# The bias of v added by a matmul in the keys phase of a two-layer gated cross-attention kernel

## The reference

```
x = x + tanh(g_xattn[0]) * attention0(layernorm(x), ctx)     # 16 heads of 16, with biases
    kh = split_heads(ctx @ w_k.T + b_k)
    vh = split_heads(ctx @ w_v.T + b_v)                       # <- this bias
x = x + tanh(g_ffn[0])   * experts(layernorm(x))
x = x + tanh(g_xattn[1]) * attention1(layernorm(x), ctx)      # 16 heads of 64, no biases
x = x + tanh(g_ffn[1])   * prototypes(layernorm(x))
```

## Time and profile before

| what | value |
|---|---|
| runs, median (lowest to highest) | 3129.29 us (3127.91 to 3131.58) |
| profiled execution: span from first to last instruction | 3124.2 us |
| what lies around the span, against the median | 5.1 us |
| keys phase, from the start of the span to the first load of the next phase | about 527 us |
| one quiet group, from v step to v step | 45.9 us |
| one noisy group | 48.4, 51.4 and 49.1 us |

### The profile page before, as it was taken

The page is one execution under the profiler, slowest core; times in us unless marked ns, Lnnn a source line. Parts: engine busy times, 40 slices in busy tenths (PEclk is TensorE's granted clock), DMA queues, the critical chain, the costliest instruction groups (busy, mean ns, idle before and its releaser), DMA issues.

```text
span 3124.2 us, 101333 instructions
## 1 busy us (share of the span) xinstructions
PE 2797.3 (90%) x33450; PEld 2225.3 (71%) x33450; DVE 2640.9 (85%) x6703; ACT 1875.0 (60%) x3733; POOL 2190.1 (70%) x3924
## 2 busy tenths in 40 slices
PE   4889896788888888869899999999999999999997
PEld 2444444666666666647688888888888888888886
DVE  6887886888888888875699999998989988999986
ACT  2666765777777777775455545555545555555553
POOL 3892001666667666645488888888888888888887
PEclk9999998999999999989999999999999999999999
DMA  5987666232223222623444444444444344444441
GB/s 153 361 332 289 244 243 227 73 86 79 73 78 83 80 74 77 224 82 81 96 104 111 107 101 95 104 104 95 101 91 97 94 103 104 96 98 93 108 94 43
DMA packets 367621, 388.79 MB, mean 124 GB/s; under 512 B 118432, under 2 KB 341264, under 8 KB 362320
## 3 DMA queue, kind: packets, MB, share of 16 engines
q1 hardware_dynamic: 346960, 335.42, 38.9%
q0 software_dynamic: 7328, 23.40, 2.4%
q10 hardware_dynamic: 12960, 25.23, 2.2%
HBM read 235.08 MB, written 148.83 MB: 123 GB/s over the span
## 4 chain that ended last, share of the span: by engine, by line
PE 39%; DVE 6%; issue 3%; POOL 2%; ACT 2%; DVEq 0%; POOLq 0%; ACTq 0%
PE banks L150 11%; PE banks L152 11%; PE banks L151 10%; PE banks L1310 2%; PE banks L1295 2%; DVE a_probT_lo L1397 1%; PE banks L1342 1%; ACT a_qT_hi L1199 1%; DVE a_pick L1522 1%; DVE a_y L1541 1%; DVE a_rsum L1409 1%; PE banks L1365 1%; DVE a_wsel L1531 0%; PE banks L1357 0%; ACT a_ynT_hi L1199 0%
## 5 line engine op out<-in xcount | busy, mean ns | idle before, releaser
L1199 ACT ACTIVATE a_qT_hi<-banks 128x512 f16<-128x512 f32 x252 | 150.5, 597 | 700.8 <-PE banks L152 700.8
L383 POOL TENSOR_TENSOR a_probT_lo<-a_expT,a_probT_hi 128x512 f16<-128x512 f32 (+1 forms) x384 | 372.0, 998 | 243.7 <-ACT a_probT_hi L458 243.7
L449 ACT ACTIVATE a_expT<-banks,a_top,w_score_scale 128x512 f32<-128x512 f32 (+1 forms) x384 | 272.2, 709 | 111.4 <-PE banks L544 111.2
L1112 POOL TENSOR_TENSOR a_pn<-a_prob,a_rsum 128x1024 f32<-128x1024 f32 (+1 forms) x256 | 307.2, 1221 | 5.8 <-DVE a_rsum L1411 5.3
L150 PE MATMUL banks<-a_xnT_hi,w_q_hi 128*128 128x256 f16 x1024 | 281.6, 275 | 4.7 <-DVE a_xnT_lo L1395 3.0
L150 PE MATMUL banks<-a_vo_front,a_probT_hi 128*128 128x256 f16 x1024 | 278.9, 272 | 2.7 <-DVE a_probT_lo L1397 2.6
L152 PE MATMUL banks<-a_xnT_hi,w_q_lo 128*128 128x256 f16 x1024 | 280.9, 274 | 0.0
L151 PE MATMUL banks<-a_xnT_lo,w_q_hi 128*128 128x256 f16 x1024 | 280.9, 274 | 0.0
L152 PE MATMUL banks<-a_vo_front,a_probT_lo 128*128 128x256 f16 x1024 | 279.0, 273 | 0.0
L151 PE MATMUL banks<-a_vo_front,a_probT_hi 128*128 128x256 f16 x1024 | 279.0, 272 | 0.0
L1397 DVE SCALAR_TENSOR_TENSOR a_probT_lo<-banks,a_probT_hi 128x512 f16<-128x512 f32 (+1 forms) x384 | 212.6, 582 | 35.7 <-ACT a_probT_hi L1199 35.3
(11 more groups left out here) (400 smaller groups left out, 10655.0 us busy)
## 6 DMA issues: line engine op xcount, KB each, us to landing
vo<-kv_vo_out SPq DMA_DIRECT2D x38, 2048.0 KB, 7.6
a_vo_front<-vo SPq DMA_DIRECT2D x128, 512.0 KB
kt<-kv_k_out ACTq DMA_DIRECT2D x9, 2560.0 KB, 15.0
a_k<-kt SPq DMA_DIRECT2D x64, 308.0 KB, 3.5
kv_raw_e<-in_L_ffn_w POOLq DMA_DIRECT2D x16, 1024.0 KB, 9.7
a_x<-in_x SPq DMA_DIRECT2D x64, 256.0 KB
a_y<-in_x SPq DMA_DIRECT2D x64, 256.0 KB, 2.8
x<-a_y SPq DMA_DIRECT2D x64, 256.0 KB, 2.2
```

What stands on the lines that cost most here:

```text
L383: pool.tensor_tensor(probT[b][1][0:rows, first:end, :], expT[b][0:rows, first:end, :], probT[b][0][0:rows, first:end, :], ALU.subtract).th ...
L449: act.activation(expT[1 - h][0:rows, first:end, :], bank, ACT.Exp, bias=top[0:rows, 0:1], scale=weights["score_scale"][0:rows, 0:1]).then_ ...
L1112: last = pool.tensor_tensor(keys_of(pn[h]), keys_of(prob_of(u, h, 2)), rsum[h][:, :].unsqueeze(2).broadcast_to([P, H, n]), ALU.mult)
L1199: act.activation(out, bank[:, 0:cols].rearrange("p (c s) -> p c s", c=out.shape[1]), ACT.Copy, scale=scale)\
```

## The change

The bias row is split once into float16 halves and put on partitions 0 (hi) and 32 (lo) of a tile `bias_parts` of 64 partitions. A second tile `pick_bias` is zero but for ones in rows 0 and 32. For each chunk a seventh matmul, `pick_bias` against `bias_parts`, with a contraction of 64 rows and 256 columns, is accumulated in the same bank, and only it signals that the bank is full. `v_sum`, its semaphore and L2279 go. ACT copies the bank, and DVE subtracts from the bank. The bank is free when the lo half is done. On DVE at the start of the phase two small operations and two waits are added; on POOL three memsets, with waits, ahead of the memset of `v_out`. PE waits once, at the first chunk of group 0, for both tiles.

```diff
-        nc.vector.tensor_scalar(bv[:, :], bv[:, :], out_inverse[:, WV:WV + 1], None, ALU.mult)
+        step(nc.vector.tensor_scalar(bv[:, :], bv[:, :], out_inverse[:, WV:WV + 1], None, ALU.mult))
+        step(nc.vector.tensor_copy(bias_parts[:, :], bv[0:64, :]))
+        nc.vector.tensor_tensor(bias_parts[32:64, :], bv[32:64, :], bias_parts[32:64, :], ALU.subtract)\
+            .then_inc(bias_ready, 1)
...
+        pool.memset(pick_bias[:, :], 0.0).then_inc(pick_zero, 1)
+        pool.wait_ge(pick_zero, 1)
+        for n, r in enumerate((0, 32)):
+            pool.memset(pick_bias[r:r + 1, :], 1.0).then_inc(pick_set, 1)
+            pool.wait_ge(pick_set, n + 1)
...
                 for c in range(DC):
-                    last = matmul3(nc, bank[0:m, 0:D], [x[:, c, a * P:a * P + m] for x in rowsT[p]],
-                                   [x[:, c, :] for x in wv], c == 0, c == DC - 1)
-                filled(last, g, ("v", a))
+                    matmul3(nc, bank[0:m, 0:D], [x[:, c, a * P:a * P + m] for x in rowsT[p]],
+                            [x[:, c, :] for x in wv], c == 0, False)
...
+                filled(nc.tensor.matmul(bank[0:m, 0:D], pick_bias[:, 0:m], bias_parts[:, :], start=False, stop=True),
+                       g, ("v", a))
...
-                need(act, v_sum_ready, g * CH + a + 1)
-                act.activation(v_out[p][0:m, a, :, :, D // H:2 * (D // H)], by_head(v_sum[0:m, :]), ACT.Copy)\
+                act.activation(v_out[p][0:m, a, :, :, D // H:2 * (D // H)], by_head(full(g, ("v", a))[0:m, 0:D]), ACT.Copy)\
                     .then_inc(v_hi, 1)
...
-                nc.vector.tensor_tensor(v_sum[0:m, :], full(g, ("v", a))[0:m, 0:D], bv[0:m, :], ALU.add)\
-                    .then_inc(v_sum_ready, 1)
-                need(dve, v_hi, at + 1)
-                need(dve, v_sum_ready, at + 1)
-                nc.vector.tensor_tensor(v_out[p][0:m, a, :, :, 0:D // H], by_head(v_sum[0:m, :]),
+                bank = full(g, ("v", a))
+                need(dve, v_hi, g * CH + a + 1)
+                nc.vector.tensor_tensor(v_out[p][0:m, a, :, :, 0:D // H], by_head(bank[0:m, 0:D]),
                                         v_out[p][0:m, a, :, :, D // H:2 * (D // H)], ALU.subtract).then_inc(v_ready, 1)
```

More of the change, by code:

```diff
@@ L1859, in keys_values_phase @@
     vT = [sb(f"vT_{n}", [P, PAIRS, BANK], F16) for n in ("hi", "lo")]
-    v_sum = sb("v_sum", [P, D])
+    bias_parts, pick_bias = sb("bias_parts", [2 * 32, D], F16), sb("pick_bias", [2 * 32, P], F16)
+    pick_zero, pick_set, bias_ready = sem("pick_zero"), sem("pick_set"), sem("bias_ready")
     work = [psum[:, s * BANK:(s + 1) * BANK] for s in range(BANKS)]
@@ L1865, in keys_values_phase @@
     vo_stored = [sem(f"vo_stored{p}") for p in range(2)]
-    rowsT_hi, rowsT_ready, k_ready, v_sum_ready, v_hi, v_ready = (
-        sem("rowsT_hi"), sem("rowsT_ready"), sem("k_ready"), sem("v_sum_ready"), sem("v_hi"), sem("v_ready"))
+    rowsT_hi, rowsT_ready, k_ready, v_hi, v_ready = (
+        sem("rowsT_hi"), sem("rowsT_ready"), sem("k_ready"), sem("v_hi"), sem("v_ready"))
     k_hi = sem("k_hi")
@@ L1928, in freed @@
             return vo_ready, (g * CH + use[1]) * PAIRS + use[2] + 1
-        return v_sum_ready, g * CH + use[1] + 1
+        return v_ready, g * CH + use[1] + 1
     def groups(eng, body):
@@ L2108, in body @@
                 for c in range(DC):
-                    last = matmul3(nc, bank[0:m, 0:D], [x[:, c, a * P:a * P + m] for x in rowsT[p]],
-                                   [x[:, c, :] for x in wv], c == 0, c == DC - 1)
-                filled(last, g, ("v", a))
+                    matmul3(nc, bank[0:m, 0:D], [x[:, c, a * P:a * P + m] for x in rowsT[p]],
+                            [x[:, c, :] for x in wv], c == 0, False)
+                if isinstance(g, int) and g == 0 and a == 0:
+                    pe.wait_ge(bias_ready, 1)
+                    pe.wait_ge(pick_set, 2)
+                filled(nc.tensor.matmul(bank[0:m, 0:D], pick_bias[:, 0:m], bias_parts[:, :], start=False, stop=True),
+                       g, ("v", a))
         first_tensor(pe)
@@ L2276, in body @@
             for a, m in enumerate(chunks(g)):
-                at = g * CH + a
-                need(dve, v_ready, at)
-                nc.vector.tensor_tensor(v_sum[0:m, :], full(g, ("v", a))[0:m, 0:D], bv[0:m, :], ALU.add)\
-                    .then_inc(v_sum_ready, 1)
-                need(dve, v_hi, at + 1)
-                need(dve, v_sum_ready, at + 1)
-                nc.vector.tensor_tensor(v_out[p][0:m, a, :, :, 0:D // H], by_head(v_sum[0:m, :]),
+                bank = full(g, ("v", a))
+                need(dve, v_hi, g * CH + a + 1)
+                nc.vector.tensor_tensor(v_out[p][0:m, a, :, :, 0:D // H], by_head(bank[0:m, 0:D]),
                                         v_out[p][0:m, a, :, :, D // H:2 * (D // H)], ALU.subtract).then_inc(v_ready, 1)
```

## The result

Seven runs of the changed kernel took 3134.81 to 3142.57 us, with a median of 3136.78 us; seven runs of the kernel before took 3121.75 to 3131.58, with a median of 3129.29. The medians are 7.5 us apart and the means 9.8. The ratio of the runs is 1.0032, with a 95% interval of 1.0021 to 1.0042: **the kernel became slower by 10.0 us (6.6 to 13.1)**. The forecast was 3134.1 us, that is +4.8. The time lies in the range given (3125 to 3141), but "same" (within 6.3 us) was given the highest chance, 0.55, and the result is beyond that mark. So the sign of the sum was right and its size about half.

A forecast was written before the change was run, and what follows sets the result against it. PE was taken as the path through v and vT, with DVE pacing the product stage. 7.9 - 0.9 - 1.3 - 1.0 + 0.1 = +4.8 us on the median 3129.3 gave 3134.1 us, range 3125 to 3141.

The forecast's parts named there:

- PE is the path from v to vT: In quiet groups' v steps, PE sets the pace and DVE's relief counts nothing; 1.31 us added per four-chunk step.
- The price of a change of height: On PE around each bias matmul, switching between 64 and 128 rows costs 0.109 us each, 0.327 per matmul.
- The rival without such a price: On PE, bias matmuls cost columns only, 3.9 instead of 11.8 us: -3.1, 3126.2 us; chance 0.17.
- DVE's stall in the noisy groups: In three groups beside POOL's work, DVE's late subtract loses 4.8 us, which the change removes; net -0.9 after bias matmuls.
- The rival of the stores: In noisy groups, store waits take back the gain: +7.0 to +10.9 us, 3136.3 to 3140.2; chance 0.30.
- noisy v stretches: Three groups beside POOL's work, v to first product split: 4.8 us gained, 3.9 of bias matmuls added, net -0.9.
- The clock: In two noisy groups, PE's clock stops falling once PE no longer waits for DVE: -1.3 us, half of 2.6.
- The tail: In the last group, the v store goes out earlier, with the last vo store as limit: -1.0 us.
- The start: At the phase's start, bias scaling and two small DVE operations mostly fit where DVE was idle: +0.1 us.
- quiet groups: Six groups with four chunks each, where bias matmuls lie wholly on PE's path: +7.9 us, period 45.9 to 47.2.

The follow-up runs named there:

- e2: The changed kernel without its bias matmul, DVE's and ACT's side kept: 3128.78 us, ratio 0.9995 to the kernel before.
- e3: The changed kernel with the bias matmul contracting 128 rows instead of 64, extra picking rows zero: 3132.05 us, ratio 1.0005 to the kernel before.
- e4: The changed kernel with a second 64-row matmul, adding zero, ahead of each chunk's six: 3146.23 us, ratio 1.0056 to the kernel before.
- e7: The kernel with v's bias folded once into the output bias, without adds, buffer or bias matmuls: 3126.97 us, ratio 0.9992 to the kernel before.
- e10: The kernel before again, unedited, timed and profiled: 3125.73 us, ratio 0.9999.
- e11: The kernel before again, unedited, for a third profile: 3126.77 us in one run.
- e5: The kernel before, DVE's add and buffer kept, plus a 64-row matmul adding zero in each chunk: 3137.72 us, ratio 1.0032.
- e1: The changed kernel once more, unedited: 3139.45 us, ratio 1.0033 to the kernel before.
- e6: The changed kernel with a group's bias matmuls in a row ahead of its v matmuls: 3136.45 us, ratio 1.0027 to the kernel before.
- e12: The kernel with v's bias folded into the output bias, unedited, profiled a second time: 3122.76 us in one run.

## Why the prediction was half right

**PE is the path from v to vT: right.** Each of the six quiet stretches grew with what PE got, 7.65 us in all (106.67 - 99.02 in the two traces), with 7.9 forecast; the period came out at 47.18 against 47.2. DVE's whole relief moved no quiet group: 99.0 in e2 as in the kernel before.

**The price of a change of height: right.** 0.21 + 0.21 = 0.42 us around a bias matmul where 0.11 + 0.11 would stand, so 0.10 for each change and 0.315 for the chunk; 0.109 and 0.327 were taken from the earlier trace rows. e3 takes the changes away and keeps the columns, e4 doubles the matmuls but not the changes, and both times follow (7.4 us less with 8 expected, 6.8 more with 6 expected). The rival without such a price (3126.2 us) is out.

On this the Trainium skill, "TensorEngine Tiling (Array Packing)", Key Properties, says that a change of tiling mode drains the engine. The trace agrees in that no weight load runs under the matmul before it there, and gives 0.10 us as the size of a change here. The rule that a matmul with few rows takes as long as a full one ("TensorE: Matmul & The Clock Gate", Why this matters for your kernels) holds for the two 64-row matmuls side by side in e4 (0.12 us) and misleads for one that stands alone between others: 0.315 us.

**DVE's stall in the noisy groups: gone, as forecast, but worth less than was put down.** It was put at -4.8 us, which against 3.9 us of bias matmuls left a net of -0.9. The stall went: L2291 is never stretched. The three v stretches give 56.9 - 52.2 = 4.7 us between the forecast's own trace and e2, and 4.0 against the mean of three traces of before, since that one execution had the largest stall. The bias matmuls put 12 x 0.32 = 3.8 back, so the net is -0.2. In time the relief without matmuls is worth 1.6 us (e2) and 2.5 us (e7); both intervals reach to 4.0, and neither alone shows that anything of it was lost.

**The rival of the stores (0.30): its time was hit, its mechanism is not shown.** It had 3136.3 to 3140.2 us, and 3136.8 was measured. By it, the stores take back in the product stages what the noisy v stretches give. Over the four traces with DVE's old chain and the expert loads (before, e10, e11, e5), product stages 0 to 3 take 121.9 us on average and at most 122.7. Over the eight with the new chain and the loads (the change, e1 to e4, e6, e7, e12; less the 1.2 in e4 and about 2.8 in e6 that bias matmuls of these kernels add in this column) they take 126.1 on average, from 121.4 to 130.8. That is 4.2 more, the size of what the v stretches gained, but two things speak against reading it as the gain taken back:

- About half of it, 2.2 us, stands in stage 0 (31.2 against 33.4), which is over before the first v step, so no gain of a v step can be taken back there.
- In stages 1 to 3 the three traces with the relief and without matmuls (e2, e7, e12) take 90.3 us, where the three of before take 90.6: nothing is taken back. The five with the new chain and with matmuls (the change, e1, e3, e4, e6) take 94.1, and e5, with matmuls and the old chain, 90.7.

Waits for stores grow with these stages (14.0 to 15.8 us in groups 0 to 3 over the four old traces, 13.5 to 20.3 over the eight new ones), and the new executions profiled were mostly long ones: five of the seven whose kernel has a median ran 2.9 to 5.8 us longer than it. So part of the 4.2 us is the choice of execution. My reason against the rival, that each store is issued by the group's own work, was weak all the same: in group 0 of e10 and e11 the product stage starts 2.5 us earlier than in the first trace and ends no earlier.

**The clock: the step that failed, with the tail.** -1.3 us was forecast, as the clock was to hold once PE no longer waited for DVE at vT. The falls of that kind are indeed gone: in 160 to 180 and in 220 to 240 us the kernel before has 0.91 and the changed one 1.00. But the clock also falls behind PE's waits for product banks, and there it falls further in the changed kernel: 0.50 in 196 to 200 us above, where the kernel before has 0.73, and 0.83 in 80 to 100 us, where it has 1.00. Over stretches of 20 us the lowest noisy values are 0.91 in the kernel before, 0.83 and 0.90 in the changed one, and 0.83 in e7, which has neither the stall nor the matmuls. What was given back in one place was lost in another, so the runs give nothing for the term of -1.3.

**The tail: wrong.** -1.0 was forecast, +0.4 measured in the changed kernel (+0.2 in e1), +0.1 in e2, from 14.69 us. The store of v is issued 1.8 us earlier and lands 2.2 us later after its issue: counted from PE's last v on it lands at 13.3 us before, 13.7 in the changed kernel and 13.4 in e2. The DMA share in the three stretches of 4 us from PE's last v on is the same in both kernels (0.97, 1.15, 0.88 before; 0.97, 1.18, 0.85 after): the last stores (1600 KB of keys, then 1024, 264 and 66 KB) keep the queues busy to the end. That an earlier store only waits in them is argued from this; no run changes these stores alone. I had counted the landing of the v store as a fixed 7.1 us.

**The start: right.** The two new operations fit where DVE was idle; the first product split moves by 3 to 4 us from one execution to the next of the same kernel, and no edit shows in it.

**The sum, by the runs:** quiet groups +7.65 (7.9 forecast), noisy v stretches -0.2 (-0.9), clock 0 (-1.3), tail +0.3 (-1.0), start 0 (+0.1): +7.75 us, where the forecast had 4.8 and 10.0 (6.6 to 13.1) was measured. The forecast was low by 5.2 us. Of these 3.3 are the gains counted for the noisy stretches, the clock and the tail that did not come, less 0.35 by which the quiet groups and the start were put too high. The other 2.25 us stand in no term of the forecast; they are within the interval, and the traces put their like in the product stages. That the measured time came out beside a rival's lower end is in part luck.

**What stays open.** Why the product stages of the changed kernel are longer, and why they take 124.4 us in e7 and 122.4 in e12, the same kernel, is not settled. PE comes to its first v step at 101.9 to 103.8 us in the four old traces and at 102.6 to 108.3 in the eight new ones. Whether the edits at the start of the phase play a part in that, or only how the first stores fall among POOL's loads in an execution, no run separates; a kernel with only those edits was not tried. Nor was one with a third buffer for the products, which would take the waits for stores away. The profile shown of the changed kernel was also that of its longest run, so its 130.8 overstates the usual case.

## What to carry to other kernels

A small matmul put between others of full height is priced by the changes of height around it: here two of 0.10 us on 0.11 us of columns, 39 times. Fill its rows up with zeros, or, better, take the term out of the loop by algebra. A stall read from one execution is worth what several executions say: here 4.8, 4.3 and 3.0 us for the same kernel. And where a stage after the edit grows by just the size of a gain, split it at the edit before calling it the place where the gain went: half of it stood ahead of the first edited step.

## What was not expected of the hardware

- The changed tail: the same 66 KB store landed in 7.1 us when it was issued late and in 9.3 us when it was issued 1.8 us earlier, behind the same 1 MB.
- A matmul of 128 rows with zeros in 64 of them is 0.21 us cheaper than one of 64 rows, between others of 128.
- PE's clock fell to half behind a wait for a store: after PE was busy for 1.51 us of 4, it was granted 1.2 GHz for the next 4 us and more, and the work behind the wait took up to twice as long (0.42 us for a key matmul instead of 0.22).
